# A graph network on one core: VectorE's comparison operands in a PSUM bank of its own, and a joined order of the one-hots

## The reference, cut to what matters

```python
xl = (x @ W_l + b_l).reshape(n, HEADS, C)            # 4 heads of 16
xr = (x @ W_r + b_r).reshape(n, HEADS, C)
e = (edge_attr @ W_e).reshape(-1, HEADS, C)
g = jax.nn.leaky_relu(xl[src] + xr[dst] + e, NEG_SLOPE)
logits = jnp.einsum('ehc,hc->eh', g, att)
amax = jax.ops.segment_max(logits, dst, num_segments=n)
ex = jnp.exp(logits - amax[dst])
denom = jax.ops.segment_sum(ex, dst, num_segments=n)
alpha = ex / (denom[dst] + 1e-16)
out = jax.ops.segment_sum(xl[src] * alpha[..., None], dst, num_segments=n).reshape(n, HEADS * C) + bias
```

## Time and profile before

| what | us |
|---|---|
| median of 3 runs | 6286.97 (6284.62 to 6289.70) |
| the profiled execution | 6286.53 |
| its span | 6284.9 |
| GpSimd, gathers of the edge loop (L733), 1568 | 1801.4 busy |
| ScalarE, windows out of PSUM (L970), 2352 | 1085.5 busy |
| VectorE, one-hots (L849, L845) | 579.2 + 381.8 busy |
| TensorE over the span | 4956.5 busy |

### The profile page before, as it was taken

How to read it: one execution, slowest core, us unless ns; L and a number is a source line. 1 busy time by engine, 2 the same in 40 slices (tenths; PEclk the granted TensorE clock), 3 DMA queues, 4 the chain that set the end, 5 groups by cost and what they waited for, 6 DMA issues and landing times. The chain is left out here.

```text
span 6284.9 us, 115432 instructions
## 1 busy us (share of the span) xinstructions
PE 4956.5 (79%) x35178; PEld 4246.0 (68%) x35178; DVE 2990.8 (48%) x4364; ACT 1854.1 (30%) x3935; POOL 3748.4 (60%) x3427
## 2 busy tenths in 40 slices
PE   2448888888888888824999957877788887884899
PEld 2335666666656666613999957777787777784899
DVE  7768888888888888737222121111111111112321
ACT  0025555555555555500000012222222222221100
POOL 7677777777777777740000047777777777776000
PEclk9668888888888888856999955555555555555799
DMA  9335555555555555523999756666667666664698
GB/s 359 104 106 160 161 162 155 159 154 158 158 157 161 155 153 161 143 49 132 367 366 365 278 157 195 208 205 210 202 197 209 206 209 208 200 200 110 254 402 327
DMA packets 622991, 1260.53 MB, mean 201 GB/s; under 512 B 131705, under 2 KB 431290, under 8 KB 597220
## 3 DMA queue, kind: packets, MB, share of 16 engines
q10 hardware_dynamic: 206000, 595.93, 30.4%
q1 hardware_dynamic: 307508, 546.42, 24.1%
q0 software_dynamic: 109184, 115.05, 8.6%
HBM read 923.85 MB, written 490.51 MB: 225 GB/s over the span
## 5 line engine op out<-in xcount | busy, mean ns | idle before, releaser
L733 POOL DMA_INDIRECT att_gl<-tab_l,top_zero x1568 | 1801.4, 1149 | 488.5 <-issue 476.1
L1217 POOL DMA_INDIRECT sum_gl<-tab_l,top_zero x1568 | 1547.1, 987 | 517.9 <-issue 477.6
L970 ACT ACTIVATE att_acc<-att_pc 128x392 bf16<-128x392 f32 x2352 | 1085.5, 497 | 1113.3 <-PE att_pc L751 984.5
L748 PE MATMUL att_pc<-att_ohl,att_ohv 128*128 128x392 bf16 x2352 | 849.1, 361 | 216.5 <-DVE att_ohl L849 216.3
L1145 PE MATMUL sum_pm<-sum_msg,sum_S 128*128 128x64 f32 x3136 | 672.2, 408 | 399.2 <-ACT sum_msg L1185 399.2
L1145 PEld LDWEIGHTS sum_pm<-sum_msg,sum_S 128*128 128x128 f32 x3136 | 646.0, 316 | 432.4 <-ACT sum_msg L1185 219.3
L751 PE MATMUL att_pc<-att_acc,att_ohv 128*128 128x392 bf16 x2352 | 843.2, 359 | 117.8 <-ACT att_acc L970 114.4
L1115 DVE TENSOR_TENSOR sum_t<-sum_pb,sum_gl 128x512 f32<-128x512 f32 x196 | 135.6, 692 | 1664.6 <-DMA sum_gl<-tab_l,top_zero 1293.8
L1127 PE MATMUL sum_pb<-sum_wbs,sum_ea 64*128 64x64 f32 x3136 | 694.8, 419 | 29.1 <-DMA sum_ea<-in_ea64T 29.1
L1127 PEld LDWEIGHTS sum_pb<-sum_wbs,sum_ea 64*128 64x128 f32 x3136 | 676.2, 329 | 40.9 <-DMA sum_ea<-in_ea64T 29.5
L767 PEld LDWEIGHTS att_pl<-att_xe,att_S 128*128 128x128 f32 x3136 | 588.0, 213 | 149.0 <-issue 125.2
(11 more groups left out here) (384 smaller groups left out, 5260.5 us busy)
## 6 DMA issues: line engine op xcount, KB each, us to landing
A<-att_acc SPq DMA_DIRECT2D x2352, 98.0 KB
l_a<-A SPq DMA_DIRECT2D x147, 1568.0 KB, 9.2
att_dall<-in_dst ACTq DMA_DIRECT2D x224, 448.0 KB
sum_dall<-in_dst ACTq DMA_DIRECT2D x196, 512.0 KB, 5.0
hop_at<-AT SPq DMA_DIRECT2D x56, 1568.0 KB
sum_a<-A ACTq DMA_DIRECT2D x49, 1568.0 KB
AT<-sum_at ACTq DMA_DIRECT2D x49, 1568.0 KB, 6.4
l_at<-AT SPq DMA_DIRECT2D x42, 1568.0 KB
```

What stands on the lines that cost most here:

```text
L733: nc.gpsimd.indirect_dma_start(out=gl[s][:, k * GQ + j, :], out_offset=None, in_=g.tab_l, in_offset=bass.IndirectOffsetOnAxis(ap=g.ix[:, c ...
L748: nc.tensor.matmul(pc[c][m % 2][:, 0:LO], ohv[c][h][:, m, :, 0], ohl[c][h][:, m // 2, :, m % 2], start=True, stop=False)
L970: nc.scalar.activation(acc[c][n % CR][:, :], pc[c][m % 2][:, 0:LO], ACT.Copy).then_inc(s_acc[c], 1)
L1217: nc.gpsimd.indirect_dma_start(out=gl[n % RB][:, j, :], out_offset=None, in_=g.tab_l, in_offset=bass.IndirectOffsetOnAxis(ap=g.ix[:, c:c + ...
```

## The change

It does five things.

1. PSUM bank `pk` belongs to VectorE. It holds `att`, the destinations of the two blocks in work (`k_dst`, copied block by block by `own_ends`), and the 16-bit column numbers (`k_lo`, 392 pairs, read as 16 bits through `k_pairs`; rows use its first 128). L836, L845, L849 and L863 read these as one operand. The transposes move into the bank of the sums (`pt = pm`).
2. The one-hots of a step are made in joined order: `ohv` and `ohl` of the first two slots for both chains, then the rest for both.
3. Because of the shared bank, `scores` waits for the evictions of the block before and stands in the next step; the sums of the third and fourth quarter both stand in the first step of a block.
4. The degrees' `ohl` is made in two pieces.
5. `root` stands ahead of the windows on ScalarE, and SP releases the scatters ahead of loading the degrees' sources.

```diff
@@ Degrees.one_hots
-                    v.tensor_tensor(
-                        t[k][:, :, :, :], spread(c[:, :, :].unsqueeze(1), [P, J // 2, w, 2]),
...
+                    pieces = ((0, J // 4), (J // 4, J // 2)) if t is self.ohl else ((0, J // 2),)
+                    for a, z in pieces:
+                        ins = v.tensor_tensor(
+                            t[k][:, a:z, :, :], spread(c[:, :, :].unsqueeze(1), [P, z - a, w, 2]),
...
+                    ins.then_inc(self.s_oh, 1)
@@ segment_ends, scalar
+                root(act)
                 act.wait_ge(s_ck, 1)
                 item_rows.windows(act)
-                root(act)
@@ expand_rows, sync
-            degrees.load(sp)
             sp.wait_ge(g.s_zero, 16 * (ZR + 2))
             sp.sem_inc(s_ix, 1)
+            degrees.load(sp)
             columns.next_windows(sp)
@@ edge_loop
-        pt = st.ps("pt", [P, 512])
+        pk = st.ps("pk", [P, 512])
         pm = st.ps("pm", [P, 512])
+        pt = pm
...
+        k_att, k_dst = pk[:, 0:D], pk[:, D:D + SL * GQ]
+        k_lo = pk[:, D + SL * GQ:D + SL * GQ + LO]
...
                 def scores(b, s):
                     wait_reuse(pe, s_xb, b)
+                    wait_reuse(pe, s_ev, b * NQ)
...
-                            if k == 0 and m == 4 and first:
+                            if k == 1 and m == 0 and first:
                                 scores(b - 1, 1 - s)
...
-                            if k < 2 and second and m in (0, 1):
-                                sums(b - 2, s, 2 + k, range(0, 4) if m == 0 else range(4, GQ))
+                            if k == 0 and second and m in (0, 1, 3, 4):
+                                sums(b - 2, s, 2 + m // 3, range(0, 4) if m % 3 == 0 else range(4, GQ))
...
+                k_pairs = k_lo.bitcast(F16).rearrange("p (l two) -> p l two", two=2)
...
+                    if k == 0:
+                        dve.wait_ge(s_kd, i * R + (s + 1))
                     v.tensor_tensor(S[s][:, k * GQ:(k + 1) * GQ, :], dall[k][:, :, :],
-                                    spread(dst[:, bass.ds(i * (R * GB) + t * GQ, GQ)].unsqueeze(2), [P, GQ, P]),
+                                    spread(k_dst[:, t * GQ:(t + 1) * GQ].unsqueeze(2), [P, GQ, P]),
                                     ALU.is_equal).then_inc(s_S, 1)
...
+                def own_ends(i, s):
+                    v.tensor_copy(k_dst[:, s * GB:(s + 1) * GB],
+                                  dst[:, bass.ds(i * (R * GB) + s * GB, GB)]).then_inc(s_kd, 1)
...
+                    v.tensor_tensor(ohv[c][h][:, 2 * a:2 * z, :, :],
+                                    spread(k_pairs[:, 0:P, :].unsqueeze(1), [P, 2 * (z - a), P, 2]),
...
+                    v.tensor_tensor(ohl[c][h][:, a:z, :, :], spread(k_pairs[:, :, :].unsqueeze(1), [P, z - a, LO, 2]),
...
-                    step(v.tensor_tensor(t2[:, :, :], t2[:, :, :], spread(att[:, :].unsqueeze(1), [P, GQ, D]),
+                    step(v.tensor_tensor(t2[:, :, :], t2[:, :, :], spread(k_att.unsqueeze(1), [P, GQ, D]),
...
-                        for c in range(CH):
-                            items(i, t, c)
+                        for a, z in ((0, 1), (1, SLOTS[t] // 2)):
+                            for c in range(CH):
+                                items(i, t, c, a, z)
...
+                        if k == NQ - 1 and not (isinstance(i, int) and i == TURNS - 1 and s == R - 1):
+                            own_ends(i if s == 0 else i + 1, 1 - s)
...
+                v.tensor_copy(k_att, att[:, :]).then_inc(s_kc, 1)
+                v.tensor_copy(k_lo, c_lo2[:, :, :].rearrange("p l two -> p (l two)").bitcast(F32)).then_inc(s_kc, 1)
...
-                            if k < 2 and second and m == 3:
-                                keep_sums(b - 2, s, 2 + k)
+                            if k == 0 and second and m in (2, 5):
+                                keep_sums(b - 2, s, 2 + m // 3)
```

More of the change, by code:

```diff
@@ L380, in turn @@
                         dve.wait_ge(self.s_hm, i * R + (k + 1 - R))
-                    v.tensor_tensor(
-                        t[k][:, :, :, :], spread(c[:, :, :].unsqueeze(1), [P, J // 2, w, 2]),
-                        spread(x[:, bass.ds(i * (R * J) + k * J, J)].rearrange("p (j two) -> p j two", two=2).unsqueeze(2),
-                               [P, J // 2, w, 2]), ALU.is_equal).then_inc(self.s_oh, 1)
+                    pieces = ((0, J // 4), (J // 4, J // 2)) if t is self.ohl else ((0, J // 2),)
+                    for a, z in pieces:
+                        ins = v.tensor_tensor(
+                            t[k][:, a:z, :, :], spread(c[:, :, :].unsqueeze(1), [P, z - a, w, 2]),
+                            spread(x[:, bass.ds(i * (R * J) + (k * J + 2 * a), 2 * (z - a))]
+                                   .rearrange("p (j two) -> p j two", two=2).unsqueeze(2), [P, z - a, w, 2]),
+                            ALU.is_equal)
+                    ins.then_inc(self.s_oh, 1)
         repeat(dve, self.HALF // (R * J), turn)
@@ L694, in edge_loop @@
             "S", "pl", "t1", "L", "LT", "sub", "exp", "back", "xb", "exm", "msg", "sum", "ev", "top"))
-        s_ends = st.sem("ends")
+        s_ends, s_kc, s_kd = (st.sem(k) for k in ("ends", "kc", "kd"))
         s_out = [st.sem(f"out{s}") for s in range(R)]
@@ L742, in item @@
                     if m == 0:
-                        pe.wait_ge(s_oh[c], i * (3 * SL) + (3 * t + 2))
+                        pe.wait_ge(s_oh[c], i * (4 * SL) + (4 * t + 2))
                     if m == 2:
-                        pe.wait_ge(s_oh[c], i * (3 * SL) + (3 * t + 3))
+                        pe.wait_ge(s_oh[c], i * (4 * SL) + (4 * t + 4))
                     if not known(n, 2):
@@ L842, in items @@
+                def items(i, t, c, a, z):
+                    h = t % 2
                     n0 = i * (CB * CJ) + (c * CI + at0[t])
-                    if not known(i, 1) or t >= 2:
+                    if a == 0 and (not known(i, 1) or t >= 2):
                         dve.wait_ge(s_mm[c], i * (CB * CJ) + (at0[t - 1] if t >= 2 else (-SLOTS[SL - 1], 0)[t]))
-                    v.tensor_tensor(ohv[c][h][:, 0:w, :, :], spread(c_row2[:, :, :].unsqueeze(1), [P, w, P, 2]),
-                                    spread(g.vals[:, bass.ds(n0, w), :].unsqueeze(2), [P, w, P, 2]), ALU.is_equal)\
-                        .then_inc(s_oh[c], 1)
@@ L848, in items @@
[L848 to L852, removed]
+                    v.tensor_tensor(ohv[c][h][:, 2 * a:2 * z, :, :],
+                                    spread(k_pairs[:, 0:P, :].unsqueeze(1), [P, 2 * (z - a), P, 2]),
+                                    spread(g.vals[:, bass.ds(n0 + 2 * a, 2 * (z - a)), :].unsqueeze(2),
+                                           [P, 2 * (z - a), P, 2]), ALU.is_equal).then_inc(s_oh[c], 1)
@@ L854, in logits @@
+                    v.tensor_tensor(ohl[c][h][:, a:z, :, :], spread(k_pairs[:, :, :].unsqueeze(1), [P, z - a, LO, 2]),
+                                    spread(g.lo[:, bass.ds(n0 + 2 * a, 2 * (z - a))]
+                                           .rearrange("p (j two) -> p j two", two=2).unsqueeze(2),
+                                           [P, z - a, LO, 2]), ALU.is_equal).then_inc(s_oh[c], 1)
                 def logits(i, n, b, s, k):
```

4 lines of the change are left out of this document (2 added, 2 removed).

## The result

The changed kernel takes 6308.49 us in the median of 20 runs, the kernel before 6277.85 beside it: a ratio of 1.0047, 95% interval [1.0039, 1.0056]. It is slower by half a per cent, where 6050 was forecast. Its profiled execution has a span of 6308.0 us.

The account below looks back on a forecast made before the run. GpSimd's gathers were taken to bound the edge loop. From 6286.5 us, 210 less in the loop and 30 less in the early stages gave 6047, said as 6050; range 5970 to 6215.

Parts of the forecast that it names:

- What bounds the kernel before: Edge loop: GpSimd's gathers and the gaps between them fill 2277.5 of 2320 us and set the pace.
- Operands in PSUM: Edge loop: four VectorE operations stop holding gathers, 284 us of 323; 16-bit operands from PSUM cost VectorE nothing.
- rivals 1 and 2: Edge loop: 16-bit PSUM reads at half rate, 6840, chance 0.14; gathers still held for 16-bit data, 6130, chance 0.08.
- More instructions on VectorE: Edge loop: smaller one-hot pieces and copies of row ends add 40 us to VectorE.
- What VectorE then allows: Edge loop: VectorE's floor of 2037 us, plus remaining waits, gives about 2110 us, 210 us less.
- the waits for TensorE shrink to a tenth: Edge loop: joined order feeds TensorE earlier, so VectorE's 183 us of waits for it fall to a tenth.
- the repairs: costed at nothing: Edge loop: later transposed scores and moved sums cost nothing; at most 38 us if TensorE's spare time is gone.
- the cover, 11 us a turn to spare: Edge loop: TensorE's spare time, 308 us in 28 turns, covers its waits for evictions.
- even with the same dip: Edge loop: with the low-clock stretch unchanged, TensorE's products need 71 us a turn, under the 73 of VectorE and GpSimd.
- Rival 3: Edge loop: TensorE's clock dips longer, VectorE keeps all 183 us of waits; total 6210, chance 0.07.
- Early stages: Ahead of the edge loop: earlier root, earlier scatter release and cut one-hots save 30 us.
- The prediction's other case, one-hots cut without use: Degrees' stage ahead of the loop: if cutting the one-hots did not help, only 15 us saved.

Follow-up runs that it names:

- Run 5: Kernel before with 8 extra, thrown-away TensorE products at the start of step 7 of each turn; the time does not move.
- run 9: Changed kernel with 8 extra TensorE products at steps 3 and 7, and the 16-bit column numbers read from SBUF again; 6157 us.
- run 12: Kernel before with the joined one-hot order alone, rows in two pieces, numbers in SBUF; 19 us slower.
- run 10: Changed kernel with message products split over two steps and 8 extra TensorE products at steps 3 and 7; 6029 us.
- Run 2: Changed kernel with 8 extra, thrown-away TensorE products at the start of steps 3 and 7 of each turn; 6041 us.
- run 7: Changed kernel with VectorE's four message products split, two moved behind the one-hots of steps 3 and 7; 6107 us.
- run 11: Kernel before with only the transposed scores in the sums' bank, two rounds later, and both sums in a block's first step; 85 us slower.
- run 1: Changed kernel whose softmax reads a constant instead of the transposed scores and does not wait for them, its numbers left out; 6101 us.
- run 8: Changed kernel with 8 extra TensorE products at the start of steps 1 and 5, where TensorE is behind; 6510 us.
- run 3: Changed kernel with only the one-hots' 16-bit column numbers read from SBUF again; ratio 1.0044 to the kernel before.

## Why the prediction was wrong

- **What bounds the kernel before** was read rightly: GpSimd. Run 5 halves the waits for TensorE and gains nothing; run 9 shows the same bound at a shorter gather (1074 ns).
- **Operands in PSUM**: right. 965 ns against 975; 16-bit numbers at the full rate (rivals 1 and 2 are out). The rule that two SBUF operands hold a gather and one in PSUM does not gave three gather times, 965, 1074 and 1149, within 10 ns. It does not account for all: for run 12 it gave some 1127, and 1160 was measured. The Trainium skill's table (VectorE: DVE Perf Modes, "The perf-mode tier table"), which gives a tensor_tensor with an operand in PSUM one element a cycle, does not hold for these shapes: 678 ns for 1024 elements a partition is 0.66 ns an element, against the 4-byte rate of 1.21 (1087 over 896).
- **More instructions on VectorE**: 40 us was too much; its busy time rose by 20 and its gaps shrank by 12.
- **What VectorE then allows**: the floor of 2037 us is about right: run 10's loop takes 2070, of which 52 are waits for TensorE. Run 2, at 2085, comes near the forecast loop of 2110, but it has products that the forecast kernel lacks. The changed kernel does not get there (2350).
- **The step that failed** is "the waits for TensorE shrink to a tenth", and below it "the repairs: costed at nothing". They rose from 199 to 345 us. Two errors are in it. First, the cover, 11 us a turn to spare, was an average over the turn. In the changed kernel TensorE waits only 4 us a turn for one-hots, all of it in steps 3 and 7, and being idle there is what lowers its clock (runs 2 and 7 take the idle time away, and falls go with it); behind a fall, in steps 0, 1, 4 and 5, it never waits for one-hots and has nothing to spare. So "even with the same dip" failed too: there are three dips in two turns instead of two. Second, the repairs were priced by what TensorE waits for an eviction (0.67 us), not by what VectorE waits for the scores that are queued two rounds of products later. The row at 940.85 has 3.31 us for it; run 11 prices the repairs alone, scores and sums together, at 85 us.
- **Rival 3** had the mechanism, a clock that is low for longer, but kept VectorE's waits at 183 where they grew by 146, by the way of the scores' wait that leads back to the dip; hence 6210 and not 6308.
- **Early stages**: 22 of the 30 us. The wait of 22.36 at L202 is 0.39 now; the first product of L286 came at 188.41 (184 forecast), for the weights; the first scatter at 218.86 (214); a scatter under the one-hots takes 1.48 to 1.70 us, every 1.8 (1.85 forecast). The prediction has VectorE's last operation close the stage; it doesn't. It starts at 339.45, 2 us earlier than before. The stage ends with the last store, in both kernels 24.2 us ahead of the loop's first S:

```profile
337.13 3.82 POOL L605 DMA_INDIRECT tab_tail<-tab_r,top_next_c  x1 [0.30 <-issue]
...
342.45 0.35 SPq L574 DMA_DIRECT2D xe<-tab_tail  x1
```

The store stood at 364.40 and came 22 us earlier, not 34: the first scatter is 5 us later than forecast, and GpSimd's last two gathers take 3.15 and 3.82 us beside VectorE's last operations. (The prediction's other case, one-hots cut without use, comes by its own numbers to 340 us and not 345; only an end of its range hangs on that.)

So the slower loop comes from the repairs, together with TensorE's clock: scores that VectorE needs stand behind a TensorE that is late after a fall, and the wait for them helps to bring the next fall. Whoever takes away that wait (run 1), the falls (run 2) or some of the idle time ahead of them (run 7) gets most of the forecast gain: 6101, 6041 and 6107 us. Three things stay open: why the second fall comes only when the repairs meet the rest of the change, what part of run 11's 85 us the move of the sums has, and the changed kernel with the scores at their old place, which was not run.

## What to carry to other kernels

Taking away the bound of one engine hands the pace to a loop of others, and what is read there must be the place, not the average: an engine with 10% to spare can be late exactly where somebody waits for it. Before moving an instruction down a queue, price the wait of whoever reads its result, with the queue in its worst stretch. If TensorE's clock falls after short idle stretches, shorten those first: by moving the work that delays it (run 7), or by products that are thrown away (run 2), but only where it idles: where it is late they cost 202 us (run 8).

## What the runs showed of the hardware

- After TensorE had stood idle for 2.76 us (up to 912.77), and for 1.25 and 1.07 us (up to 955.00 and 957.19), its granted clock fell from 2.4 to 1.2 GHz (1.00 to 0.50) and stayed there for 17.0 us, in which it was busy for 16.8. 16 products a turn, thrown away, at steps 3 and 7 kept the loop's granted clock at 0.99 and cut TensorE's busy time by 216 us. The same products at steps 1 and 5 gave 0.79.
- In this loop a fall helps to bring the next: late products (912.77 on), a waiting VectorE (3.13, 1.78 and 3.31 us), late one-hots, an idle TensorE (957.19), the next fall. With the wait for the scores cut (run 1) the clock is 0.91 instead of 0.84.
- VectorE compared 16-bit numbers with one operand in PSUM as fast as with both in SBUF: 413 ns for 512 elements a partition, 678 for 1024, 960 for 1568, against 418, 681 and 965 in run 3.
- With the one-hots' numbers in PSUM GpSimd's gathers took 965 ns on average, with these numbers in SBUF 1074 (run 3).
